# Layer 2 attention begun with half of the queries: two of four chunks are gathered, normalised and multiplied inside its steps

## The reference, cut to what matters

```python
x = x + _L0_xattn_ref(_layernorm(x), ctx, ctx, ...)   # windows of 128 tokens, 16 heads of 16
x = x + _L0_ffn_ref(_layernorm(x), ...)               # 16 experts, top 2, and a shared expert
x = x + _L1_xattn_ref(_layernorm(x), ctx, ...)        # each group of 256 tokens against its 256 keys
x = x + _L1_ffn_ref(_layernorm(x), ...)               # 8 experts, top 2
```

```python
qh = (q @ Wq.T + bq); kh = (kv @ Wk.T + bk); vh = (kv @ Wv.T + bv)
attn = softmax(einsum('bqhd,bkhd->bhqk', qh, kh) * scale)
out = einsum('bhqk,bkhd->bqhd', attn, vh) @ Wo.T + bo
```

## Time and profile before

| what | value |
|---|---|
| timed runs | 902.91 us median of 3 (902.14, 902.91, 909.47) |
| profiled execution, span from first to last instruction | 917.2 us |
| PE, DVE, ACT, POOL busy | 811.1, 591.5, 401.2, 213.6 us |
| last product of layer 0's experts to first scores of the second attention | 394 to 493 us |
| steps of the second attention | 493 to 618 us |

### The profile page before, as it was taken

One profiled execution on the slowest core, in us unless ns is written; L12 is line 12 of the kernel. 1 busy time (PEld: TensorE's weight loads), 2 busy tenths in 40 slices (PEclk: granted clock), 3 DMA queues, 4 the chain that ended last, 5 costly groups with the idle time before them and its releaser, 6 DMA issues.

```text
span 917.2 us, 23713 instructions
## 1 busy us (share of the span) xinstructions
PE 811.1 (88%) x8698; PEld 602.5 (66%) x8699; DVE 591.5 (64%) x1391; ACT 401.2 (44%) x768; POOL 213.6 (23%) x185
## 2 busy tenths in 40 slices
PE   4879999799979999985689999998979999999994
PEld 3545555465648888853344666656449999999993
DVE  3345778768956677724565788869965555555562
ACT  3243556554232333320332666666874444444440
POOL 0004000100013333257012000001023444444432
PEclk9989999999999999997797999999999999999997
DMA  8865431305363333366235523229533333343331
GB/s 267 131 83 63 64 101 31 132 16 191 107 223 102 97 109 102 100 125 139 39 46 70 72 95 119 69 70 326 160 124 60 63 70 65 68 71 65 65 59 24
DMA packets 74593, 91.32 MB, mean 100 GB/s; under 512 B 15520, under 2 KB 60448, under 8 KB 74528
## 3 DMA queue, kind: packets, MB, share of 16 engines
q1 hardware_dynamic: 59600, 63.09, 28.3%
q0 software_dynamic: 13008, 25.97, 12.3%
q10 hardware_dynamic: 1920, 1.34, 0.5%
HBM read 60.86 MB, written 17.56 MB: 86 GB/s over the span
## 4 chain that ended last, share of the span: by engine, by line
PE 68%; DVE 12%; issue 8%; ACT 5%; DMA 3%; another core or an unknown queue 2%; SPq 1%; POOLq 0%; DVEq 0%; ACTq 0%
PE bank L955 18%; PE bank L968 14%; PE bank L717 5%; PE bank L862 3%; PE bank L738 3%; PE bank L686 3%; PE bank L578 3%; PE bank L534 3%; PE bank L940 3%; PE bank L874 2%; DVE neg_max L1458 2%; PE bank L549 2%; PE bank L704 2%; DVE arena L1755 2%
## 5 line engine op out<-in xcount | busy, mean ns | idle before, releaser
L968 PE MATMUL bank<-arena 128*128 x1218 | 279.4, 273 | 4.0 <-DVE arena L1768 2.2
L1326 ACT ACTIVATE arena<-bank,router_b 128x128 f32<-128x128 f32 x312 | 86.8, 375 | 124.0 <-DMA router_b<-in_exp_b 109.2
L1458 DVE TENSOR_REDUCE neg_max<-bank 128x2 f32<-128x512 f32 (+1 forms) x180 | 117.5, 685 | 28.5 <-PE bank L686 28.3
L968 PEld LDWEIGHTS bank<-arena 128*128 128x128 f16 x1218 | 119.0, 98 | 11.9 <-issue 10.3
L955 PE MATMUL bank<-att,arena 128*128 128x128 f16 x960 | 104.6, 219 | 2.7 <-issue 2.7
L1156 ACT ACTIVATE arena<-bank 128x1024 f32<-128x1024 f32 x96 | 96.7, 1026 | 15.7 <-PE bank L704 15.0
L955 PE MATMUL bank<-attT,arena 128*128 128x128 f16 x912 | 99.3, 219 | 0.0
L955 PE MATMUL bank<-arena 128*128 128x128 f16 x1128 | 97.2, 222 | 2.0 <-DVE arena L1760 2.0
L955 PEld LDWEIGHTS bank<-att,arena 128*128 x960 | 91.8, 98 | 8.7 <-issue 3.3
L1938 POOL DMA_INDIRECT out<-arena,put_i x39 | 65.9, 1691 | 110.2 <-DVE arena L1781 96.1
L955 PEld LDWEIGHTS bank<-attT,arena 128*128 x912 | 86.5, 98 | 5.6
(11 more groups left out here) (216 smaller groups left out, 1359.8 us busy)
## 6 DMA issues: line engine op xcount, KB each, us to landing
arena<-arena SPq DMA_DIRECT2D x96, 128.0 KB, 4.8
arena<-in_exp_up SPq DMA_DIRECT2D x16, 512.0 KB, 3.7
y_d<-arena SPq DMA_DIRECT2D x47, 128.0 KB, 1.7
arena<-in_exp_dn SPq DMA_DIRECT2D x5, 1024.0 KB, 6.0
arena<-in_exp_up SPq DMA_DIRECT2D x5, 1024.0 KB, 5.1
arena<-in_exp_b SPq DMA_DIRECT2D x39, 128.0 KB
arena<-in_ctxT SPq DMA_DIRECT2D x8, 512.0 KB, 7.1
arena<-in_exp_dn SPq DMA_DIRECT2D x16, 256.0 KB, 4.0
```

The costliest lines, as they stand in the source:

```text
L968: last = mm(yP[u], hidT[u][x][:, k], weights(e, 1, w, k * D, D), start=n == 0, stop=n == n_second - 1)
L1326: last = fn(hid[:, k * P:(k + 1) * P], upP[u][:, half, (k % 4) * P:(k % 4 + 1) * P], ACT.Relu, bias=b1_col[u][:, k:k + 1], scale=1 / WS)
L1458: v.tensor_reduce(neg_max[u][:, column(m * HM):column(m * HM) + 2 * HM - 1:2], mx[m % 2].rearrange("p (h k) -> p h k", h=HM), AX.X, ALU.ma ...
```

## The change

Keys of all chunks have a buffer of their own, so ACT no longer waits for the stack DMAs. The order of `project(1)` is: all keys and values, and the queries of chunks 0 and 1 alone (`SOON[1] = 2`); the first maxima and the first step wait for these two. POOL gathers chunks 0 and 1, waits until the stack of query chunk 0 has landed, and then gathers chunk 2, adds the bias to chunks 0 and 1, combines chunk 2 itself (`combine_late`), gathers and combines chunk 3. The rest of the query work of chunks 2 and 3 stands in the steps: statistics in steps 1 and 4, writing of `xn` in 2 and 5, the turn in 3 and 6, the product and its cuts in 4 and 7. SP stacks query chunks 1, 2 and 3 after placing the shifts of tiles 0, 5 and 8, and the first two weight loads follow. The loops of ACT and DVE over the steps are written out for this layer.

```diff
+    SOON = [4, 2]
+    LATE_STATS, LATE_APPLY = {1: 2, 4: 3}, {2: 2, 5: 3}
+    LATE_TURN, LATE_QUERIES = {3: 2, 6: 3}, {4: 2, 7: 3}
...
+        k_homes = [[arena[:, 16384 + 1024 * u:17408 + 1024 * u] for u in range(2)] * 2,
+                   [arena[:, 16384:17408], arena[:, 17408:18432], arena4[:, 2048:3072], att_w[:, 0:2].rearrange("p w k d -> p (w k d)")]]
...
+        lateP = bank[:, 2:4]
...
@@ SP, project and attend @@
                     keys(1, 0)
                     keys(1, 1)
+                    keys(1, 2)
                     queries(1, 0)
-                    queries(1, 1)
+                    keys(1, 3)
...
                         if i == 0:
-                            keys(1, 2)
-                        if i == 1:
+                            queries(1, 1)
+                        if i == 5:
                             queries(1, 2)
-                        if i == 2:
-                            keys(1, 3)
-                        if i == 3:
+                            sp.wait_ge(s["x_ffn"], 3)
+                            load_weights1(0)
+                        if i == 7:
+                            sp.wait_ge(s["x_ffn"], 6)
+                            load_weights1(1)
+                        if i == 8:
                             queries(1, 3)
-                        if i == 5:
-                            sp.wait_ge(B[0]["x_ffn"], T)
+                        if i == 9:
                             sp.wait_ge(s["q_mm"], NC)
-                            load_weights1(0)
-                        if i in (7, 9, 10, 11, 14):
-                            load_weights1({7: 1, 9: 2, 10: 4, 11: 5, 14: 3}[i])
+                        if i in (9, 10, 11, 14):
+                            load_weights1({9: 2, 10: 4, 11: 5, 14: 3}[i])
...
@@ PE, project @@
                     keys(2)
+                    values(2)
                     turn_tokens(0, 0)
-                    values(2)
+                    values(3, 0, TC // 2)
                     queries(0, 0)
+                    values(3, TC // 2, TC)
                     keys(3)
                     turn_tokens(1, 1)
-                    values(3)
+                    first_maxima(l, 0, 2)
                     queries(1, 1)
-                    turn_tokens(2, 0)
-                    queries(2, 0)
-                    turn_tokens(3, 1)
-                    first_maxima(l, 0, 2)
-                    queries(NC - 1, 1)
                     first_maxima(l, 2, 8)
                     turn_first(l)
...
@@ PE, attend @@
+                    if l and p == 0 and i - 1 in LATE_TURN:
+                        pe.wait_ge(s["xT_ready"], LATE_TURN[i - 1] + 1)
+                    if l and p == 0 and i - 1 in LATE_QUERIES:
+                        pe.wait_ge(s["qparts_ready"], LATE_QUERIES[i - 1] + 1)
...
+                def late_turn(i, c):
+                    pe.wait_ge(s["xn_ready"], c + 1)
+                    pe.wait_ge(s["exp_done"], i * NP + NP - 1)
...
+                def late_queries(i, c):
+                    pe.wait_ge(s["xT_ready"], c + 1)
+                    pe.wait_ge(s["exp_done"], i * NP + NP - 1)
...
+                    if l and i in LATE_TURN:
+                        late_turn(i, LATE_TURN[i])
+                    if l and i in LATE_QUERIES:
+                        late_queries(i, LATE_QUERIES[i])
                     values(i, u, 0)
...
@@ ACT, project and attend @@
                     keys(1)
-                    root(0)
                     values(1)
                     keys(2)
+                    values(2)
+                    root(0)
                     turned(0, 0)
+                    queries(0)
+                    values(3)
                     root(1)
-                    values(2)
-                    queries(0)
                     keys(3)
                     turned(1, 1)
...
                         if p == max(NP - 2, 1) and not first:
                             copy_attention(i - 1)
+                    if l and isinstance(i, int) and i in LATE_TURN:
+                        late_turned(LATE_TURN[i])
+                    if l and isinstance(i, int) and i in LATE_QUERIES:
+                        late_queries(LATE_QUERIES[i])
+                    if l and isinstance(i, int) and i in LATE_STATS:
+                        late_root(LATE_STATS[i])
...
@@ DVE, project and attend @@
                     keys(0)
                     output_bias()
-                    prepare(0, 0, lambda: keys(1))
-                    prepare(1, 1, lambda: keys(2))
-                    prepare(2, 0, lambda: queries(0))
+                    keys(1)
+                    prepare(0, 0)
+                    keys(2)
+                    prepare(1, 1, lambda: queries(0))
                     keys(3)
-                    prepare(3, 1, lambda: queries(1))
-                    queries(2)
...
                         add(i - 1)
+                    if l and i in LATE_QUERIES:
+                        late_queries(LATE_QUERIES[i])
                     if left > 1:
                         maxima(i + 2, u, SPREAD[l][2 * KW + 1], NM)
+                    if l and i in LATE_STATS:
+                        late_stats(LATE_STATS[i])
+                    if l and i in LATE_APPLY:
+                        late_apply(LATE_APPLY[i])
...
@@ POOL @@
+            def combine_late(c):
+                s, done = B[1], 3 * (c - SOON[1])
...
+                pool.tensor_tensor(y, y, gates[...], ALU.mult).then_inc(s["x_ffn"], 1)
+                pool.tensor_tensor(y[:, 0], y[:, 0], y[:, 1], ALU.add).then_inc(s["x_ffn"], 1)
+                pool.tensor_tensor(x_res[:, of_chunk], x_res[:, of_chunk], y[:, 0], ALU.add).then_inc(s["x_ffn"], 1)
...
+                    pool.wait_ge(s["q_in"][0], STACKS * 16)
+                    gather_results(2)
+                    add_bias(0, 0)
+                    add_bias(1, 1)
+                    combine_late(2)
+                    gather_results(3)
+                    combine_late(3)
+                    add_bias(2, 0)
+                    add_bias(3, 1)
```

More of the change, by code:

```diff
@@ L561, in turn_tokens, with values @@
                     last.then_inc(s["tr_mm"], 1)
-                def values(c):
-                    after(pe, s["v_ready"], c)
-                    for t in range(TC):
+                def values(c, lo=0, hi=TC):
+                    if lo == 0:
+                        after(pe, s["v_ready"], c)
+                    for t in range(lo, hi):
                         for k in range(KD):
@@ L1349, in _, with cut_rest, late_stats, late_apply @@
             own = [Steps(dve, B[l]["step"]) for l in range(2)]
[L1350 removed]
+            routing = [Steps(dve, B[l]["chunk_step"], SOON[l] * 3) for l in range(2)]
+            late = own[1]
+            def cut_rest(parts, f, bias, s_ready):
+                for m in range(KD):
+                    last = v.scalar_tensor_tensor(out=parts[:, 1, m], in0=f[:, m], scalar=bias[:, m:m + 1], in1=parts[:, 0, m],
+                                                  op0=ALU.add, op1=ALU.subtract)
+                last.then_inc(s_ready, 1)
+            def late_stats(c):
+                dve.wait_ge(B[1]["x_ffn"], 3 * (c - 1))
+                for t in range(TC):
+                    last = v.bn_stats(stats[:, t], x_res[:, c * TC + t])
+                late.then(last)
+                for t in range(TC):
+                    last = v.bn_aggr(mean_var[:, t], stats[:, t])
+                late.then(last)
+                v.tensor_scalar(var_eps[:], mean_var[:, :, 1], EPS, None, ALU.add).then_inc(B[1]["var_ready"], 1)
+            def late_apply(c):
+                dve.wait_ge(B[1]["sd_ready"], c + 1)
+                late.then(v.reciprocal(rstd[:], std[:]))
+                dve.wait_ge(B[1]["tr_mm"], c - 1)
+                for t in range(TC):
+                    last = v.tensor_scalar(xn[c % 2][:, t], x_res[:, c * TC + t], mean_var[:, t, 0:1], rstd[:, t:t + 1], ALU.subtract, ALU.mult)
+                last.then_inc(B[1]["xn_ready"], 1)
+            def late_queries(c):
+                dve.wait_ge(B[1]["q_hi"], c + 1)
+                cut_rest(q_parts[c % 2], lateP, bqk[:, 0], B[1]["qparts_ready"])
             def normalise(l, c, u, chain, n, free):
@@ L1370, in project @@
                 s = B[l]
-                def cut_rest(parts, f, bias, s_ready):
-                    for m in range(KD):
-                        last = v.scalar_tensor_tensor(out=parts[:, 1, m], in0=f[:, m], scalar=bias[:, m:m + 1], in1=parts[:, 0, m],
-                                                      op0=ALU.add, op1=ALU.subtract)
-                    last.then_inc(s_ready, 1)
                 chain = Steps(dve, s["chunk_step"])
@@ L1534, in attend @@
                 maxima(1, 1, 0, NM)
-                in_all_pairs(dve, T, step, 2)
+                if l == 0:
+                    in_all_pairs(dve, T, step, 2)
+                else:
+                    for i in range(T):
+                        step(i, i % 2)
```

101 lines of the change are left out of this document (66 added, 35 removed).

## The result

The changed kernel takes 925.34 us (median of 4 executions, 922.41 to 929.58), the kernel before beside it 904.79 (902.14 to 909.47): a ratio of 1.0224, 95% interval 1.0159 to 1.029. It is slower, as forecast, but by 20.5 us in place of 10.2, and lies above the range of 894 to 920. Ratios are of executions in the fast state alone, so they need not equal the quotient of the medians printed. Of the executions of after the profile shows one of 928.07 us, span 926.2; so 1.9 us lie outside the span, not the 4.8 that I had worked out.

The account below looks back on a forecast made before the run. The prediction took POOL's gathers to set the stage before the steps and PE to bound the steps; 902.9 - 12.3 + 22.5 = 913.1 us, with a range of 894 to 920.

Parts of the forecast that it names:

- The front: Stage before the second attention's steps: first scores at 461.8 against 474.1, a gain of 12.3 us.
- The base: First profile of before: ACT's 15.73 us gather wait taken as absent from timed runs, 4.8 us outside the span.
- Sum 22.5 us: Second attention's steps: everything the change adds to steps 1 to 7 and tile 9's shift, 22.5 us.
- The terms with a late product: Steps 4 and 5 (8.4 and 1.6 us) and step 7 (5.3 us): late query products, statistics and normalising.
- the shift of step 9: SP's queue: tile 9's shift waits behind the query stack, costing 0.4 us.
- The turn alone: Steps 3 and 6: eight transposes on PE and a longer exp wait, 1.25 us each.
- the root terms: Late roots ahead of ACT's raw copy: 3.1 us, and 3.1 within the 8.4; bounds 0 to 2 x 4.6.
- the likeliest case: Whole kernel as worked out: 913.1 us, spanning 906 to 919 from the root terms' bounds; chance 0.47.
- B, the wait is real: Gathers: they hold other engines in timed runs too, so the gain is 31.4 and time 894.0 us; chance 0.20.
- C, the late work is hidden: Steps: roots and cuts fall in idle ACT and DVE time, adding 11.5 us, total 902.1; chance 0.20.
- D, the clock: Steps 2 and 5: pauses bring one more half-clock stretch each, about 7 us, total 920; chance 0.10.
- E, the drain: Steps: four table switches with 1.38 us drain each add 5.5 us, total 918.6; chance 0.03.

Follow-up runs that it names:

- before_again: The kernel before, unchanged, profiled a second time on the first chip: 905.23 us, span 903.4.
- slot_root: Changed kernel with the late root moved into ACT's pause of steps 2 and 5, a tiny exp behind it: 929.88 us, ratio 1.0128.
- sp_order: Changed kernel with SP's first weight load behind tile 6's shift and query chunk 3's stack behind tile 9's shift: 936.48 us, ratio 1.0169.
- soon3: Changed kernel with only chunk 3 late, root in ACT's pause, all gathers at once, better queue order: 933.41 us, ratio 1.0119; soon3_pair, third chip: 934.13 us, 1.0161.
- order_only: Kernel before with own key buffers and keys and values first, all four query chunks still ahead of the steps: 910.33 us, ratio 1.0078.
- after_pair: The changed kernel, unchanged, run on the third chip: 938.98 us, one execution, 1.021 times the median of before there.
- root_copy: Changed kernel with a plain copy in place of the two late square roots, so no table switch: 924.64 us, ratio 1.0203.
- both: Changed kernel with the root in ACT's pause of steps 2 and 5 and SP's queue in the new order: 937.4 us, ratio 1.0161.
- fill_wait: Changed kernel with ten unread PE products in each of two pauses ahead of the steps: 942.03 us, ratio 1.0224.
- hollow: Changed kernel with late work of query chunks 2 and 3 cut to small instructions, waits, gathers and DMAs kept: 911.34 us, ratio 1.0043.

## Why the prediction was right and wrong

**The balance.** From before_again to after the spans differ by 22.8 us. Front -12.3; steps +33.9; tail +5.2; and the end of layer 0, which the change leaves alone, came 4.1 earlier in this execution (first keys at 392.76 against 396.86). In sum 22.7.

**The front was right,** 12.3 forecast and 12.3 measured. Both absolute times were 4.6 us longer than I had them (first scores 80.2 and 67.9 after the first keys by the prediction, 84.8 and 72.5 in the profiles), and this fell out of the difference. That the two misses are equal is luck in part: each front has a query product at half clock that neither working had (6.45 us from 451.04 in before_again, 5.58 from 442.07 in after, for 3.67).

**The base was read wrongly, without harm.** I took the first profile to be an execution with a wait that timed runs lack, and put 4.8 us outside the span. It is 1.8 to 1.9, as in every run here: 917.2 + 1.9 = 919.1 is what the kernel before takes on a chip that has the wait. The timed runs of 902.91 are too short to have had it.

**The step that failed is "Sum 22.5 us", what the change adds to the steps: it measured 33.9.** By its terms, each against before_again:

| part | forecast | after |
|---|---|---|
| step 0 | 0 | 2.3 |
| steps 1 and 2: statistics, root | 3.1 | 8.5 |
| step 3: writes and turn | 1.2 + 1.25 | 3.6 |
| steps 4 and 5 | 8.4 + 1.6 | 10.6 |
| step 6 | 1.25 | 2.3 |
| step 7 | 5.3 | 5.2 |
| step 9 | 0.4 | 1.4 |

(The writes of the normalised chunk stand behind the turn of the maxima, so what I called step 2's shows in step 3.) The terms with a late product were right in sum, 15.3 forecast and 15.8 measured, though step 5 had 0.74 of the clock, which the terms did not have. Of the 11.4 us too few, 6.8 are steps 0 and 1, which the sum had at nothing beyond the root: they are the granted clock, shown by step 1 with late statistics in it at 7.6 in the four profiles where the clock was back (slot_root, sp_order, soon3, soon3_pair) and at 11.2 to 12.9 in five where it wasn't. The remaining 4.6 are smaller misses of each term: statistics and root 4.0 for 3.1, writes and turn 3.6 for 2.45 (2.4 at full clock in slot_root), step 6, and the shift of step 9, for which I had let the stack of copies cost almost nothing. The turn alone, 1.25 by the prediction, measured 2.3 in step 6 at full clock.

As an estimate over all steps: after spends 37.7 us of them at half clock (23.9 from 466.4, 3.4 from 497.1, 3.5 from 507.3, 6.9 from 531.2), before_again 6.9. Half of the difference, 15.4 us, is the most that the clock can have cost. PE's own late work is 9.5, and at least 9.0 of the 33.9 are waits between the engines.

Two bounds of the prediction were also misread. By its own bounds of 0 to 9.2 for the root terms the likeliest case ends at 916, not 919. And a step 0 at full clock lasts 9.0 us (order_only), not 7.6, so the 14 us shown there held at most 5.0 of half clock, not 6.4.

**Outside the sum** stand 5.2 us of the tail, a term that the prediction did not have at all. Nothing of the change is there, but the same instructions run in part at half clock. The router stage and the experts of before_again, and then of after (stretches, columns as above):

```profile
611.50:669.20 57.70, 49.55 (x264) 28.96 (x263) 49.86 (x138) 45.74 (x37) 7.42 (x7) 1.00 0.65 217
```

```profile
629.00:690.30 61.30, 54.02 (x263) 32.25 (x262) 49.94 (x138) 45.74 (x37) 7.42 (x7) 0.92 0.61 204
```

3.6 us of the 5.2 are in this stage. All three profiles of before have a tail of 291.9; of eleven profiles of changed versions only slot_root's has, the others 292.7 to 300.5; soon3 on two chips has 294.5 and 294.6. (after and after_pair have 297.1 and 295.3). So it seems to go with the kernel rather than with chance, but what in a kernel sets it was not found.

**The rivals.** *B, the wait is real:* after's profile doesn't have it, and the timed runs beside it (904.79) are too short for it; on two chips it is real, ends with the gathers in before as B says, and the front gains 16.9 for 12.3. B's 31.4 are reached nowhere, since after keeps 11.5 us of the wait for its own two chunks. *C, the late work is hidden:* refuted, no late step with a product is under 12.7. *D, the clock:* came true as an addition to the first case, with 0.10 too small a chance. Steps 2 and 5 have the stretches that D named (3.4 and 6.9 us), and step 2 loses its own when the root leaves the step's boundary. But the largest is at the start of the steps, where before has one too, so that D's 7 us agree with the 6.8 of steps 0 and 1 by chance. In before step 0 lasts 11.7 to 13.8 us, against the 9.0 of a step 0 at full clock (order_only, soon3); in after the stretch is longer. *E, the drain:* refuted. In sp_order the row at 497.98 is a load of 1.28 us and the exp begins at 499.27, 0.01 behind it. (root_copy, with no late loads, has after's time, but its interval could not tell the 5.5 us of E from none.) The Trainium skill, "ScalarE: Activation LUTs", section "What ACT_TABLE_LOAD costs", adds 1.38 us of drain to a switch; no row here has it.

**Not settled:** why the stretch at half clock from the start of the steps lasts 24 us in after, after_pair, both and fill_wait (27 in root_copy) and 10 in sp_order, slot_root and hollow, the code of steps 0 and 1 being the same in after and sp_order. What ACT waits for in the gathers of two of the chips isn't settled either; the profile names no releaser.

## What to carry to other kernels

Work moved out of a waiting front into steps in which PE is the bound is paid in full there, and with interest: each late product cost 5.1 to 5.2 us for its 3.67, since PE, ACT and DVE hand over in turn behind it (PE busy 11.09 of 12.70 us). Put a late operation that two engines wait for (a root between table loads) into the pause of its engine, not at a step's boundary: it took at least 3 us off step 2, though step 5 showed no such gain in slot_root and 2.6 us in both, and no gain in the whole time is clear of the noise. Check that a filling is no longer than the pause it is to fill. And before a wait without a cause in one profile is set aside or counted, take a second profile on another chip.

## What the runs showed of the hardware

- One kernel, 905 us on one chip and 920 on two others, by a wait of ACT during POOL's indirect gathers that every profile of the two has and no profile of the first. It was 15.0 to 15.7 us behind 32 gathers, 10.7 to 11.7 behind 16, and 32.8 in two pieces in soon3 and soon3_pair, where keys and values come first and all 32 gathers run beside them. In each of these profiles the landings of SP's copies are missing from the records of that time. What ACT waits for is not known.
- PE's clock fell to half while PE was busy. In after it was granted 1.00 for the 10 us up to the first step, PE busy 8.61 of them, then 0.54 in step 0 with PE busy 13.22 of 14.00:

```profile
455.30:465.30 10.00, 8.61 (x39) 3.71 (x38) 6.92 (x11) 0.00 (x0) 9.70 (x5) 1.00 0.48 68
```

- Ten of eleven profiles of changed versions have 0.8 to 8.6 us more in a tail that the edits leave alone. Their stretches at half clock there lie between 616 and 710 us (one of 20.5 us in hollow, PE busy throughout), and before and slot_root have none there. What in a version brings them about was not found.
- A shift of two small DMAs lands 5.08 us after its issue when six stack copies stand ahead of it in the queue (after, 566.45).
